# A memset after every row gather in both attention loops of a four-layer graph network, and constant waits in the counted layer

## The chip, the core and the metric

The kernel runs on one core of a Trainium2 chip. The metric is the device time of one execution in microseconds. The engines are TensorE (PE in the profile, PEld for its weight loads), VectorE (DVE), ScalarE (ACT), GpSimd (POOL) and SyncE (SP), each with an instruction stream of its own, in order, synchronised by semaphores.

## The reference, cut to what matters

Four graph layers, each on a layer-normed copy of x and added back to it. There are 3125 nodes with 128 features, and 103125 edges (50000 in both directions and a loop at each node), sorted by destination. Layer 0 is a two-step graph convolution, layer 3 filters 64 edge attributes and multiplies them with gathered rows. The change touches the loops of layers 1 and 2, and one place in layer 0.

```python
def reference(x, src, dst, edge_attr_64, ...):
    edge_index = jnp.stack([src, dst])
    h = jnp.maximum(_layernorm(x, axis=-1), 0.0)
    x = x + _L0_gnn_ref(h, edge_index, ...)
    ...
    x = x + _L1_gnn_ref(h, edge_index, ...)
    ...
    x = x + _L2_gnn_ref(h, edge_index, ...)
    ...
    x = x + _L3_gnn_ref(h, edge_attr_64, src, dst, ...)
    return x

def _L1_gnn_ref(x, edge_index, W, att):
    ...
    projected = (x @ W).reshape(N, HEADS, OUT_CH)
    src = projected[row]
    dst = projected[col]
    scores = jnp.tanh(src + dst)
    scores = jnp.einsum('ehc,hc->eh', scores, att)
    scores = jnp.exp(scores - jnp.max(scores, axis=0, keepdims=True))
    out = jax.ops.segment_sum(src * scores[:, :, None], col, num_segments=N)
    normalizer = jax.ops.segment_sum(scores, col, num_segments=N)
    out = out / jnp.maximum(normalizer, 1e-12)[:, :, None]
    ...

def _L2_gnn_ref(x, edge_index, gamma, beta, Wl, bl, Wr, br, att, res_W, bias):
    ...
    xl = (h @ Wl + bl).reshape(n, H, D)
    xr = (h @ Wr + br).reshape(n, H, D)
    src, dst = (edge_index[0], edge_index[1])
    e = jax.nn.leaky_relu(xl[src] + xr[dst], NEG_SLOPE)
    alpha = jnp.einsum('ehd,hd->eh', e, att)
    alpha = _segment_softmax(alpha, dst, n)
    msg = xl[src] * alpha[..., None]
    out = jax.ops.segment_sum(msg, dst, num_segments=n)
    ...
```

## The kernel before

The edges are cut into 202 tiles of 512 (`k.tiles`), each of four sub-tiles of 128 (`SUB`), one edge to a partition. The stages follow each other: the count matrices of layer 0 are built, layer 0 is computed from them (`sum_counted`), then come the additive attention of layer 1 and the GAT attention of layer 2 (both by `attend`), and the filtered scatter of layer 3 (`scatter_filtered`) with its dense layers.

**`attend`.** The projected node features lie in a table in HBM. GpSimd's block is unrolled (L2069 to L2073): for each tile it waits until a slot of the ring is free (`sums_ready`, `n + 1 - ring`) and then runs `gather` (L892), which issues four indirect DMAs, one per sub-tile, each of 128 rows by the source indices (L897). Each counts up its own semaphore `rows_loaded[slot][j]`. The ring has 12 slots in layer 1 (rows of 128 features) and 8 in layer 2 (rows of 256 features: two heads). The slots are tiles whose names differ, so the profile calls the target of a gather `gathered`, `wide` or `h_nm`. TensorE turns the gathered rows (L2088), adds the destination's features from a window of the table by a one-hot matrix (L2092), and ScalarE applies tanh (L2172) or a copy (L2170), in layer 2 followed by VectorE's leaky relu (L2221). TensorE forms the scores (L2109 in layer 1, L2106 in layer 2) and, beforehand, the cells' mask (L2101); VectorE takes the maximum of each row (L2228, L2230, in layer 2 also L2235), ScalarE the exponential (L2178), TensorE turns the weights back (L2119), VectorE copies them (L2246), and TensorE multiplies them with the gathered rows into the sums of each node in the tile's window (L2144 in layer 1, L2140 in layer 2), which counts up `sums_ready`. The sums are copied by ScalarE (L2190, or L2184 in layer 2, where TensorE turns them with L2152). VectorE makes the one-hot matrices (L1477); SyncE loads the destinations (L1457) and the windows (L1462). Each engine's order is written out, and its loop runs ahead of the others only as far as the semaphores let it.

**`sum_counted`.** The count matrices lie in HBM (`k.all_counts`), built in an earlier stage. One tile of them is built again here before the sums begin; the number of such rounds is `k.rebuild`, here 1. SyncE loads the first group of 24 matrices in three thirds, then stores the rebuilt tile (L1378), and then loads the next groups (L1390). TensorE multiplies each group with the features (L1195), 25 blocks of nodes; for the first group it waits for the thirds one by one.

**`scatter_filtered`** has for each sub-tile one indirect DMA that adds rows (L1709), 606 in all, each with a `sem_inc` and a wait of GpSimd ahead of it.

## Time and profile before

| | us |
|---|---|
| timed runs | 4901.65, 4906.43, 4910.76 |
| median | 4906.43 |
| span of the profiled execution | 4898.1 |
| busy in it: TensorE, VectorE, GpSimd, ScalarE | 3999.0, 2847.4, 2828.1, 1737.4 |
| from the first gather of layer 1 (668.90) to the end of its last | 1222.6 |
| from the first gather of layer 2 (2023.53) to the end of its last | 1305.4 |

The spans and busy times are of one profiled execution, the timed runs are others; the profiled span lies 8.3 us under their median. A row of the timeline gives start, duration, engine, line, operation, output and input, and in brackets how long the engine was idle before it and what ended that (`<-`); "issue" is the engine's own work between instructions, "remote" a semaphore event whose sender the profile could not name, and a release can also be put down to a DMA that happened to end then. Granted clock is TensorE's, as a share of its full 2.4 GHz.

### The profile page before, as it was taken

The page shows a single profiled execution, that of the slowest core. Times are in us where ns is not written, and L with a number is a line of the kernel's source. Part 1 is how long each engine was busy: PE and PEld are TensorE (multiplying, and loading weights), DVE is VectorE, ACT ScalarE, POOL GpSimd, SP SyncE. Part 2 cuts the span into 40 slices and gives each one's busy share as a digit, 9 for nine tenths or more (in the row PEclk, how much of TensorE's full clock was granted, in tenths as well). Part 3 has the DMA queues.
Part 4 walks back from the last instruction along what each step waited for, and adds up shares of the span by engine and source line. Part 5 has one row for each costly group of instructions (what it writes and reads, how often), then busy time and mean ns, then how long its engine had stood idle before and what let it go on. Part 6 is the DMA issues. An engine that isn't in the chain of part 4 may idle for free. (4 is left out here: it accounts for less than half of the span.)

```text
span 4898.1 us, 89702 instructions
## 1 busy us (share of the span) xinstructions
PE 3999.0 (82%) x22566; PEld 2260.3 (46%) x22566; DVE 2847.4 (58%) x8457; ACT 1737.4 (35%) x4474; POOL 2828.1 (58%) x3060
## 2 busy tenths in 40 slices
PE   3997927788887877488888888885399999999987
PEld 1344414445544544344444444442256655556652
DVE  7994032333333334555555555556678888888868
ACT  3773023344344334333333333331322222222227
POOL 0122356666666663555555555554368888888862
PEclk8998957776777777688988888886699999999999
DMA  2333422222222221333333333330056666666650
GB/s 80 91 87 103 147 71 57 57 56 57 57 56 57 56 57 27 113 98 96 97 97 96 96 97 96 97 96 18 21 97 104 105 105 104 104 105 104 104 110 13
DMA packets 377425, 402.41 MB, mean 82 GB/s; under 512 B 86457, under 2 KB 322502, under 8 KB 377030
## 3 DMA queue, kind: packets, MB, share of 16 engines
q0 software_dynamic: 151904, 198.72, 21.0%
q1 hardware_dynamic: 225382, 202.21, 14.4%
q8 instruction: 43, 0.70, 0.1%
q14 instruction: 96, 0.79, 0.1%
HBM read 312.91 MB, written 87.78 MB: 82 GB/s over the span
## 5 line engine op out<-in xcount | busy, mean ns | idle before, releaser
L897 POOL DMA_INDIRECT gathered<-table,sources x952 | 903.6, 949 | 600.6 <-issue 259.9
L1709 POOL DMA_INDIRECT sums<-gathered,idx x606 | 988.7, 1632 | 217.8 <-issue 166.4
L1571 PE MATMUL bank<-wide 128*128 128x512 bf16 x3636 | 851.5, 379 | 0.0
L2228 DVE TENSOR_REDUCE neg_raw<-bank 80x1 f32<-80x512 f32 (+1 forms) x404 | 276.6, 685 | 725.9 <-remote 252.1
L897 POOL DMA_INDIRECT wide<-table,sources x464 | 438.7, 946 | 275.1 <-issue 125.7
L1571 PEld LDWEIGHTS bank<-wide 128*128 128x128 bf16 x3636 | 347.7, 98 | 364.1 <-issue 1.7
L2178 ACT ACTIVATE msg<-bank,neg_top 80x512 f32<-80x512 f32 (+1 forms) x404 | 275.7, 682 | 643.1 <-DVE neg_top L2230 353.6
L1222 POOL TENSOR_TENSOR acc<-acc,msg 128x20 f32 x404 | 108.3, 268 | 411.2 <-issue 244.6
L2221 DVE TENSOR_TENSOR zact<-zact,bank 128x512 f32<-128x512 f32 x404 | 259.5, 683 | 123.1 <-ACT zact L2170 72.9
L2106 PE MATMUL bank<-zact,att_cells 128*32 128x512 f32 x808 | 289.4, 732 | 37.9 <-issue 36.2
L2088 PEld LDWEIGHTS bank<-ident,gathered 128*128 128x128 f32 x1360 | 191.8, 165 | 258.0 <-issue 232.2
L2109 PE MATMUL bank<-zact,att_cells 128*80 128x512 f32 x404 | 301.6, 838 | 6.6 <-issue 6.6
L2246 DVE COPY edge_rows<-bank 128x320 f32<-128x320 f32 (+1 forms) x404 | 183.2, 453 | 203.5 <-remote 132.7
L2144 PE MATMUL bank<-edge_rows,gathered 128*128 128x80 f32 x1088 | 193.9, 337 | 92.5 <-DVE edge_rows L2246 81.9
L2088 PE MATMUL bank<-ident,gathered 128*128 128x128 f32 x1360 | 237.4, 317 | 35.4 <-issue 26.4
L2119 PE MATMUL bank<-ident,msg 80*128 80x80 f32 (+1 forms) x1616 | 215.5, 262 | 61.5 <-issue 33.9
L897 POOL DMA_INDIRECT h_nm<-table,sources x200 | 189.4, 947 | 130.5 <-DMA wide<-table,sources 69.3
L2190 ACT COPY partial<-bank 32x20 f32 (+1 forms) x808 | 132.6, 164 | 357.5 <-remote 239.5
L1169 DVE TENSOR_SCALAR gathered<-iota_c,partial 128x500 f16<-128x500 f16 x808 | 257.6, 339 | 1.7 <-issue 1.3
L2170 ACT ACTIVATE zact<-bank 128x512 f32<-128x512 f32 x404 | 216.8, 588 | 98.1 <-DMA window<-parts 81.2
L1178 PE MATMUL bank<-gathered,zact 128*128 128x500 f16 x812 | 209.3, 381 | 49.4 <-ACT zact L1285 28.1
L1622 ACT COPY gathered<-bank 128x437 f32<-128x437 f32 x202 | 106.1, 525 | 337.0 <-PE bank L1597 249.7
(406 smaller groups left out, 7603.9 us busy)
## 6 DMA issues: line engine op xcount, KB each, us to landing
zact<-in_src_flat SPq DMA_DIRECT2D x202, 192.0 KB
edge_rows<-in_attr_rows SPq DMA_DIRECT2D x202, 128.0 KB
dst_pair<-local_rows SPq DMA_DIRECT2D x177, 128.0 KB
gathered<-table,sources POOLq DMA_INDIRECT x952
dst_pair<-local_rows SPq DMA_DIRECT2D x202, 64.0 KB
counts<-wide SPq DMA_DIRECT2D x4, 3000.0 KB
counts<-fm_ab SPq DMA_DIRECT2D x4, 3000.0 KB
fm_ab<-counts SPq DMA_DIRECT2D x4, 3000.0 KB, 11.0
```

Of the source, the lines that this page charges most:

```text
L897: pool.indirect_dma_start(out=g[:, j, :], out_offset=None, in_=table, in_offset=bass.IndirectOffsetOnAxis(ap=mine, axis=0)).then_inc(rows_ ...
L1169: hot = dve.tensor_scalar(k.cell_hot[slot][:, j, :], k.iota_c[:, :], own, None, ALU.is_equal)
L1571: pe.matmul(k.bank[b][:, :], k.split[t.two][:, c, :], k.source_hot[t.two][:, b * CHUNK:(b + 1) * CHUNK], start=first, stop=c == PARTS - 1, ...
L1709: pool.indirect_dma_start(out=k.sums[j], out_offset=bass.IndirectOffsetOnAxis(ap=k.idx[t.slot][:, j:j + 1], axis=0), in_=out_rows(t)[:, j, ...
L2088: pe.matmul(z_bank(t, h)[:, j * P:(j + 1) * P], g[:, j, h * F:(h + 1) * F], k.ident[:, :], is_transpose=True, start=(j == 0), stop=False, ...
L2106: mm = pe.matmul(score_bank(t)[own_cells(h), :], a.att[h][:, own_cells(h)], k.zact[t.two][:, h, :], start=False, stop=True, skip_group_che ...
L2109: mm = pe.matmul(score_bank(t), a.att[0][:, :], k.zact[t.two][:, 0, :], start=False, stop=True)
L2119: mm = pe.transpose(weight_bank(t)[:, j * cells:(j + 1) * cells], raised(t)[:, j * P:(j + 1) * P], k.ident[lanes(t), lanes(t)])
L2170: act.mul(k.zact[t.two][:, h, :], z_bank(t, h)[:, :], 0.2).then_inc(slope_ready, 1)
L2178: act.activation(raised(t), score_bank(t), ACT.Exp, bias=k.neg_top[lanes(t), bass.ds(t.t, 1)], accum_out=k.weight_sum[lanes(t), bass.ds(t. ...
L2221: m = dve.tensor_tensor(za, za, z_bank(t, h)[:, :], ALU.max)
L2228: dve.tensor_reduce(raw, score_bank(t), AX.X, ALU.max, negate=True).then_inc(top_found, 1)
```

## The change

First, both attention loops hand `gather` a new semaphore `paused`. After each of the four indirect DMAs of a tile GpSimd now sets one of eight columns of a new tile `pause` (128x8, fp16), which nothing reads, to zero, and counts `paused` up; from the third tile on, `gather` first waits for the memsets of the tile two before, which wrote the same columns. It adds 4 memsets a tile, 808 to each loop. `gather` has no other callers.

Second, in `sum_counted` SyncE loads only the first two thirds inside the loop of rebuilt tiles, waits at the loop's end for the second of them, and loads the third after the loop. TensorE waits inside its loop for the first third, then for a new semaphore `second_there` and for a count of 16, where it waited against `k.rebuild * 16 + 16`, a register's value.

```diff
@@ gather
-def gather(k, pool, table, g, gathers_begun, rows_loaded, t):
+def gather(k, pool, table, g, gathers_begun, rows_loaded, t, paused=None):
 
     pool.sem_inc(gathers_begun, 1)
+    if paused and t.t > 1:
+        pool.wait_ge(paused, (t.t - 1) * SUB)
     for j in range(SUB):
         mine = k.sources[:, t.t * SUB + j:t.t * SUB + j + 1]
         pool.indirect_dma_start(out=g[:, j, :], out_offset=None, in_=table,
                                 in_offset=bass.IndirectOffsetOnAxis(ap=mine, axis=0)
                                 ).then_inc(rows_loaded[t.slot][j], 16)
+        if paused:
+            at = t.t % 2 * SUB + j
+            pool.memset(k.pause[:, at:at + 1], 0.0).then_inc(paused, 1)
@@ sum_counted, SyncE
-                    for landed in begun:
+                    for landed in begun[0:2]:
                         sp.sem_inc(landed, 16)
+
+                    def load_third(i):
+                        lo, hi = thirds[i]
+                        sp.dma_start(k.counts[0][:, lo:hi, :], k.all_counts[lo:hi, :, :].rearrange(
+                            "t p c -> p t c")).then_inc(begun[i], 16)
                     with sp.Fori(0, k.rebuild) as n:
-                        for (lo, hi), landed in zip(thirds, begun):
-                            sp.wait_ge(landed, n * 16 + 16)
-                            sp.dma_start(k.counts[0][:, lo:hi, :], k.all_counts[lo:hi, :, :].rearrange(
-                                "t p c -> p t c")).then_inc(landed, 16)
+                        for i in range(2):
+                            sp.wait_ge(begun[i], n * 16 + 16)
+                            load_third(i)
                         sp.wait_ge(evicted, n + 1)
...
                         sp.wait_ge(stored, n * 16 + 16)
                         sp.sem_inc(free, 1)
+                        sp.wait_ge(begun[1], n * 16 + 32)
+                        sp.sem_inc(rounds_done, 1)
+                    sp.sem_inc(second_there, 1)
+                    load_third(2)
@@ sum_counted, TensorE
                         cell_counts(k, pe, 0, k.bank[0]).then_inc(counted, 1)
+                        pe.wait_ge(begun[0], n * 16 + 32)
...
                         for i, (lo, hi) in enumerate(thirds if first(now) else [(0, now.size)]):
-                            if first(now):
-                                pe.wait_ge(begun[i], k.rebuild * 16 + 16)
+                            if first(now) and i == 1:
+                                pe.wait_ge(second_there, 1)
+                            if first(now) and i == 2:
+                                pe.wait_ge(begun[2], 16)
@@ attend
+        paused = st.sem("paused")
...
-                    gather(k, pool, table, rows(t), gathers_begun, rows_loaded, t)
+                    gather(k, pool, table, rows(t), gathers_begun, rows_loaded, t, paused)
```

GpSimd's instructions in the additive loop before, where the ring goes from one set of slots to the next. The name in brackets is that of an earlier holder of the same semaphore: `parts0_rounded2` is `sums_ready` here.

```order
716 L897 DMA gathered<-table,sources 128x128 [waits parts0_rounded2]
717 L897 DMA gathered<-table,sources 128x128 x3
718 L897 DMA wide<-table,sources 128x128 [waits parts0_rounded2]
719 L897 DMA wide<-table,sources 128x128 x3
720 L897 DMA wide<-table,sources 128x128 [waits parts0_rounded2]
721 L897 DMA wide<-table,sources 128x128 x3
```

The same loop after the change; `parts0_rounded0` is `sums_ready`, `build_low_ready` is `paused`.

```order
820 L900 DMA gathered<-table,sources 128x128 [waits parts0_rounded0,build_low_ready]
821 L905 MEMSET pause 128x1
822 L900 DMA gathered<-table,sources 128x128
823 L905 MEMSET pause 128x1
824 L900 DMA gathered<-table,sources 128x128
825 L905 MEMSET pause 128x1
826 L900 DMA gathered<-table,sources 128x128
827 L905 MEMSET pause 128x1
828 L900 DMA gathered<-table,sources 128x128 [waits parts0_rounded0,build_low_ready]
```

Each gather, the last of a tile too, is followed by one memset, and the two waits stand together before a tile's first gather.

SyncE's instructions at the rebuild loop of `sum_counted` before (L1375 the thirds, L1378 the store, L1390 the next group).

```order
48 L1375 DMA wide<-counts 128x8x500 [waits counted_begun0]
49 L1375 DMA wide<-counts 128x8x500 [waits counted_begun1]
50 L1375 DMA wide<-counts 128x8x500 [waits counted_begun2]
51 L1377 REGISTER_ALU
52 L1378 ISA [waits counted_evicted]
53 L1378 DMA counts<-fm_ab 128x500
54 L1372 REGISTER_ALU [waits counted_stored]
55 L1372 COMPARE_AND_BRANCH
56 L1390 DMA fm_ab<-counts 128x24x500
```

And after it (L1382 the thirds, L1389 the store, L1405 the next group):

```order
48 L1382 DMA wide<-counts 128x8x500 [waits counted_begun0]
49 L1382 DMA wide<-counts 128x8x500 [waits counted_begun1]
50 L1388 REGISTER_ALU
51 L1389 ISA [waits counted_evicted]
52 L1389 DMA counts<-fm_ab 128x500
53 L1393 REGISTER_ALU [waits counted_stored]
54 L1384 REGISTER_ALU [waits counted_begun1]
55 L1384 COMPARE_AND_BRANCH
56 L1382 DMA wide<-counts 128x8x500
57 L1405 DMA fm_ab<-counts 128x24x500
```

The third load has moved from before the store to behind the loop, directly ahead of the next group's load.

## Rows read from the trace of the kernel before

**Rows 1.** The page, its first line.
```profile
span 4898.1 us, 89702 instructions
```

**Rows 2.** Windows: length, busy us (instructions) of PE, PEld, DVE, ACT, POOL, granted clock, DMA share, GB/s.
```profile
668.90:1891.53 1222.63, 965.56 (x4112) 582.91 (x4113) 392.16 (x1255) 472.89 (x1465) 766.40 (x808) 0.72 0.22 57
2020.00:3330.00 1310.00, 1081.83 (x7479) 567.60 (x7480) 722.54 (x1977) 406.80 (x994) 765.76 (x809) 0.86 0.33 96
3700.00:4600.00 900.00, 900.00 (x5429) 540.30 (x5428) 738.27 (x1861) 264.57 (x621) 758.26 (x466) 1.00 0.65 104
```

**Rows 3.** The timeline of GpSimd, first and last gather of the GAT loop.
```profile
2023.53 1.54 POOL L897 DMA_INDIRECT gathered<-table,sources  x1 [3.10 <-POOLq L539]
...
3328.03 0.94 POOL L897 DMA_INDIRECT gathered<-table,sources  x1 [0.30 <-issue]
```

**Rows 4.** The page, groups: count | busy us, mean ns | idle us before, releaser.
```profile
L897 POOL DMA_INDIRECT gathered<-table,sources x952 | 903.6, 949 | 600.6 <-issue 259.9
...
L897 POOL DMA_INDIRECT wide<-table,sources x464 | 438.7, 946 | 275.1 <-issue 125.7
...
L897 POOL DMA_INDIRECT h_nm<-table,sources x200 | 189.4, 947 | 130.5 <-DMA wide<-table,sources 69.3
```

**Rows 5.** The timeline at the opening of the additive loop.
```profile
708.58 0.77 PE L2119 MATMUL bank<-ident,msg 80*128 80x80 f32 x4 [5.49 <-issue]
...
732.82 0.49 DVE L2246 COPY edge_rows<-bank 128x320 f32<-128x320 f32 x1 [25.19 <-remote]
```

**Rows 6.** The timeline of a burst in the additive loop.
```profile
1320.67 1.09 PE L2109 MATMUL bank<-zact,att_cells 128*80 128x512 f32 x2
...
1327.61 0.94 POOL L897 DMA_INDIRECT gathered<-table,sources  x1 [0.30 <-issue]
1328.73 0.69 DVE L2228 TENSOR_REDUCE neg_raw<-bank 80x1 f32<-80x512 f32 x1 [8.48 <-remote]
...
1331.79 0.94 POOL L897 DMA_INDIRECT gathered<-table,sources  x1 [3.23 <-remote]
```

**Rows 7.** The timeline of a burst in the GAT loop.
```profile
2146.62 1.07 PE L2140 MATMUL bank<-gathered,edge_rows 128*32 128x128 f32 x16
...
2149.75 0.95 POOL L897 DMA_INDIRECT gathered<-table,sources  x1 [0.30 <-issue]
...
2151.81 0.26 ACT L2184 COPY tile_rows<-bank 64x128 f32<-64x128 f32 x1 [3.39 <-DMA wide<-table,sources]
```

**Rows 8.** The timeline in the scatter stage of the last layer.
```profile
3998.25 0.91 PE L1597 MATMUL bank<-msg,gathered 128*128 128x128 f32 x6
...
3999.20 0.53 ACT L1622 COPY gathered<-bank 128x437 f32<-128x437 f32 x1 [1.54 <-PE bank L1597]
```

**Rows 9.** The timeline of GpSimd in the prologue.
```profile
0.35 0.10 POOL L3154 MEMSET const-float32-0.0<- 128x1 f32 x1
0.38 0.10 POOL L3154 MEMSET const-float32-1.0<- 128x1 f32 x1
```

**Rows 10.** A window of 7 us in the additive loop, columns as in rows 2.
```profile
1204.00:1211.00 7.00, 7.00 (x23) 3.98 (x23) 0.02 (x1) 2.52 (x6) 5.48 (x6) 0.50 0.21 56
```

**Rows 11.** The timeline of TensorE in that window.
```profile
1204.59 1.99 PE L2109 MATMUL bank<-zact,att_cells 128*80 128x512 f32 x2
...
1210.91 2.00 PE L2109 MATMUL bank<-zact,att_cells 128*80 128x512 f32 x2
```

**Rows 12.** The timeline at the start of the counted sums.
```profile
465.09 0.37 SPq L1390 DMA_DIRECT2D fm_ab<-counts  x1
465.17 0.45 PE L1195 MATMUL bank<-wide,h_nm 128*128 128x160 f16 x2 [6.74 <-SPq L1387]
...
482.82 0.56 ACT L1210 COPY msg<-bank 128x480 f32<-128x480 f32 x1 [23.78 <-PE bank L1195]
```

**Rows 13.** DMA issues of that stage: count, KB each, median us to landing.
```profile
wide<-counts SPq DMA_DIRECT2D x3, 1000.0 KB, 7.7
```

**Rows 14.** The one-hots of the GAT loop: duration min/median/max in ns, first and last start.
```profile
L1477 DVE TENSOR_SCALAR onehot_t<-dst_pair,iota_w,always x97: 398/413/620, 2204.3 to 3191.3; 128x512 bf16<-128x512 bf16 x97
```

More of the change, by code:

```diff
@@ L309, in load_everything @@
     k.att1 = k.sb("att1", [F, HEADS1])
+    k.pause = k.sb("pause", [P, 2 * SUB], FP16)
     one, two = k.soft1, k.soft2
@@ L1356, in one_pass @@
             loaded, begun = [st.sem(f"loaded{i}") for i in range(2)], [st.sem(f"begun{i}") for i in range(3)]
+            second_there, rounds_done = st.sem("second_there"), st.sem("rounds_done")
             summed, kept, adds_begun, added = st.sem("summed"), st.sem("kept"), st.sem("adds_begun"), st.sem("added")
```

## Prediction, made before the changed kernel ran

> **What bounds the kernel now.** The page gives the span, 4898.1 us [rows 1]; the median of the three timed runs is 4906.43, so 8.3 us lie outside the profiled span, and I add them at the end. The stretches come next [rows 2]. The additive loop takes 1222.6 us and the GAT loop 1305.4 us (2023.53 to the end of its last gather at 3328.97 [rows 3]), together 52% of the span. In neither is an engine full: TensorE is busy 965.56 of 1222.63 and 1081.83 of 1310.00 us, GpSimd 766.40 and 765.76. In the last layer's edge stage it is 900.00 of 900.00. So the two loops wait on something, and only they are touched by the memset.
>
> The groups of the page show what GpSimd could do [rows 4]. The 1616 gathers of both loops take 949, 946 and 947 ns each. Before one that follows another without a wait there are 0.30 us of issue [rows 3]. So a gather costs 1.25 us, a tile of four 5.0 us, and 808 gathers 1010 us. The idle time before them is 600.6 + 275.1 + 130.5 = 1006.2 us; less 1616 x 0.30 = 485 it leaves 521 us of waiting. By loop: 1222.6 - 1010 = 212 and 1305.4 - 1010 = 295, 507 in all; the rest lies before the first gather of each loop and in rounding.
>
> What GpSimd waits for is `sums_ready`, the signal that TensorE has finished with a slot of gathered rows. TensorE is not late with its work; its signals are late. At the opening of the additive loop 12 tiles, 48 gathers, run without a wait from 668.9 to 668.9 + 48 x 1.25 = 729. TensorE ends the four turns of the first weights (L2119) at 708.58 + 0.77 = 709.35; the copy that needs just these (DVE L2246) starts at 732.82, 23.5 us later, 3.8 us after the burst's end [rows 5]. In the steady loop the score matmul L2109 ends at 1321.76, the maximum that reads it (DVE L2228) starts at 1328.73, again just after the last gather of a burst (1328.55), and GpSimd itself waits 3.23 us more [rows 6]. In the GAT loop L2140 ends at 2147.69, its copy on ScalarE starts at 2151.81, 1.1 us after the burst of gathers ended at 2150.70 [rows 7]. In the scatter stage it is not so: L1597 ends at 3999.16 and ScalarE's copy of it starts at 3999.20 [rows 8], while scatters go out all the time. There a `sem_inc` and a wait stand before each scatter, and 466 of them in 900 us are 1.93 us apart [rows 2]. My reading: a run of gathers without a break holds TensorE's signals up, the consumers idle, and their lateness stops GpSimd in turn. That this is the run of gathers and not the gathers as such is inferred from these four places.
>
> **The memset, part by part.** It adds 808 memsets of 128x1 to each loop, 1616 in all, and before each tile from the third on a wait for memsets of the tile two before; those are older on the same in-order engine, so that wait is met when it is reached, and the queue behind it (the gathers, for which TensorE's feature transposes wait) is not held by it. The nearest rows for a memset are those of the prologue: 0.10 us long, the next one starting 0.03 later [rows 9]. I bound the added GpSimd time by these: 1616 x 0.03 = 48 us, 1616 x 0.10 = 162 us. I take 0.10, since a memset between two gathers has no second memset to overlap; a gather then costs 1.35, a tile 5.4 us, a loop 1091 us. The Trainium skill (Perfetto Trace Analysis, Per-instruction lifecycle) says that a GpSimd instruction's span in a profile is unreliable and that it is to be timed by the start-to-start spacing; by that, the price is the 0.03, and the added time 48 us. No row here has a memset between gathers, so the sum keeps both ends. Neither end is below nothing by itself; the gain can only come through the signals.
>
> If the signals become prompt, GpSimd is the bound: additive 1222.6 - 1091 = 132 us, GAT 1305.4 - 1091 = 214 us, 346 us together. Two things take from that. First TensorE's clock in the additive loop: granted 0.72 on average [rows 2], and where it is at its low level, 1.2 GHz, granted 0.50, a tile of TensorE takes 6.32 us, 1204.59 to 1210.91 [rows 10, 11], more than the 5.4 of GpSimd; the loop goes between the levels. The full clock would carry it, the low one not, and I see no row that says that the share of either changes. I take half of the 132, about 70 us. Second the GAT loop: TensorE is busy 1081.83 us of it at 0.86, just under 1091, so small stalls on either engine no longer hide behind the other. I take 175 of the 214. Sum: 70 + 175 = 245 us.
>
> **The mend in the counted layer** is run once here (`k.rebuild` is 1). Before, SyncE issues all three thirds of the first counts, then stores the rebuilt tile. After it, the third one goes out after the store has landed, just before the next group's load at 465.09, and TensorE's start at 465.17 stands behind one more issue and one semaphore step, some 0.4 us by the 0.37 of such an issue [rows 12]. A third is 1000 KB and lands in 7.7 us [rows 13]: at 465.2 + 7.7 = 473. TensorE works the first group from 465.17 to about 482.8, where ScalarE's copy starts after its wait [rows 12], 17.6 us, so it wants the last third after two thirds of that, 11.7 us, at 477. Four us of cover; were it gone, the loss is what lands late, and twice the landing time would still cost under 4 us. The new waits of TensorE for loads that landed long before cost nothing. I take 1 us. So 245 - 1 = 244: span 4654, time 4654 + 8.3 = 4662.
>
> **Rivals.**
> A. *No relief, longer bursts.* The memset is again GpSimd work, and if the signals come only when GpSimd's queue stops, each burst just grows. The cycle is then burst plus gap, as in rows 5 to 7, where signals came 1 to 4 us after the burst's end, and each gather's memset stands in it: 1616 x 0.03 = +48 (4954), 1616 x 0.10 = +162 (5068). This is the side that loses; it decides if the held signals come out of order with the gathers only in GpSimd's waits. For it: the 0.30 us of issue between two gathers are a gap already three times as long as the memset, and they don't let the signals out. Against it: that gap is the same instruction stream preparing the next gather, whereas a memset is work of another kind; the scatters at 1.93 us with their own step before each hold nothing up [rows 8].
> B. *Relief paid back in full.* A memset must be started and finished between gathers; if that costs 0.3 us, as an issue does, a tile is 4 x 1.55 = 6.2 us, a loop 1252: additive +30, GAT -53, together -23 with prompt signals, nothing to speak of; at 0.35 exactly zero. Within 0.2%: 4897 to 4916.
> C. *Partial relief.* The signals come out at some memsets, the bursts of the opening break up, and a third to a half of the waits go: 4760 to 4890.
> D. *Vector shuts GpSimd out.* The memset wants to write SBUF while DVE runs its one-hot in bf16, 0.41 us each [rows 14], 404 of them; if each held up GpSimd fully, +166 beyond A, 5234. Against: the same DVE instructions already run beside the gathers, whose means are 949, 946 and 947 ns with nothing added. The Trainium skill (SBUF, Who interferes with whom) says that DVE in a 2-port mode and GpSimd lock each other out, and that a GpSimd DMA's descriptor writes are held too; the trace shows no such stretch in the gathers.
>
> **How the numbers follow.** Prompt signals with GpSimd near its bound: .45, at 4662, with a range of its own from 4550 (346 us and a memset of 0.10) to 4760. C .12; B, with the case that the memset does nothing at all, .10; A .30; D or something dearer .03. Below 4550 the memset would have to be 0.03 with nothing lost to the clock. The likeliest is 4662. The range must leave out no more than 2 in 10, and A has .30 in it, so it goes to A's end: 4550 to 5070. A measurement of this kernel tells about 0.2% from no change, 10 us. Faster .57, same .10, slower .33.
>
> **What would show it.** In the trace after: the start-to-start of two gathers with a memset between them (1.35 by me; 1.28, 1.55 or more by the others) and the waiting before gathers (521 us to nearly nothing; unchanged in A). DVE L2246 in the opening of the additive loop no longer 23 us behind L2119; L2228 and ScalarE's L2184 within some tenths of TensorE's end. The loops' lengths, 1150 and 1130 us by me. The granted clock of the additive loop: if it falls below 0.72 while GpSimd waits for real, my half was too much. Rows in which the signals are prompt and GpSimd still waits would put the bound elsewhere. The counted layer's first matmul within 1 us of 465.2. My number is wrong above all if a memset is no break for the signals.

## The result, and the profile after

The changed kernel took 4912.69 us (median of 18 runs) against 4904.99 us of the kernel before (18 runs): a ratio of 1.0016, 95% interval [1.001, 1.0022]. It is 0.16% slower, which is no change by the 0.2% of the prediction. The forecast of 4662 us was wrong; the direction it gave .57 to did not come.

The windows of the changed kernel over its two loops (columns as in rows 2, each from about the first gather to the last memset):

```profile
span 4902.5 us, 91319 instructions
```
```profile
668.00:1889.00 1221.00, 921.39 (x4092) 553.97 (x4093) 391.44 (x1249) 470.81 (x1460) 863.60 (x1616) 0.76 0.22 57
2024.00:3336.00 1312.00, 1079.26 (x7484) 568.57 (x7485) 721.31 (x1974) 406.87 (x994) 865.73 (x1616) 0.86 0.33 96
```

All 1616 memsets ran, 808 in each loop, and the loops took 1221 and 1312 us where they had taken 1222.6 and 1305.4 [rows 2, 3]. The groups of GpSimd's gathers (page), which answer rows 4:

```profile
L900 POOL DMA_INDIRECT gathered<-table,sources x952 | 903.8, 949 | 478.0 <-issue 151.5
...
L900 POOL DMA_INDIRECT wide<-table,sources x464 | 438.9, 946 | 224.0 <-issue 75.2
...
L900 POOL DMA_INDIRECT h_nm<-table,sources x200 | 189.2, 946 | 108.8 <-DMA wide<-table,sources 71.3
```

The idle time before the gathers is 478.0 + 224.0 + 108.8 = 811 us instead of 1006. The 195 us between them are the memsets, not less waiting. GpSimd's timeline in a stretch without waits shows it:

```profile
673.80 0.94 POOL L900 DMA_INDIRECT gathered<-table,sources  x1 [0.19 <-issue]
674.74 0.13 POOL L905 MEMSET pause<- 128x1 f16 x1
675.05 0.94 POOL L900 DMA_INDIRECT gathered<-table,sources  x1 [0.19 <-issue]
```

Two gathers start 1.25 us apart, as before. The memset takes 0.12 us of the 0.30 us that lay between two gathers anyway, and 0.18 stay. Here it is neither a cost nor a pause. That holds for nearly all gathers, not for every one: within a tile the gathers of this trace start 1.265 us (additive loop) and 1.268 us (GAT loop) apart on average, against 1.261 and 1.262 before. Some of the stretched ones lie in the opening burst, where each of the five gathers from 701.3 on has the next one only 1.4 to 2.1 us later, though no wait for `sums_ready` stands there yet:

```profile
703.29 0.94 POOL L900 DMA_INDIRECT gathered<-table,sources  x1 [0.81 <-issue]
...
705.39 0.94 POOL L900 DMA_INDIRECT gathered<-table,sources  x1 [0.81 <-POOL pause L905]
```

The second one is put down to the memset, that is to `paused`. At the opening of the additive loop TensorE's signals are still late:

```profile
690.79 0.69 PE L2138 MATMUL bank<-ident,msg 80*128 80x80 f32 x4
...
707.72 0.77 PE L2138 MATMUL bank<-ident,msg 80*128 80x80 f32 x4 [5.49 <-issue]
...
716.65 0.49 DVE L2265 COPY edge_rows<-bank 128x320 f32<-128x320 f32 x1 [9.89 <-remote]
```

The copy at 716.65 is the first of the loop, and it waits for the first turns alone. Those are the turns at 690.79, which end at 691.48; the ones at 707.72 are the second tile's, which TensorE may do ahead. So the first signal comes 716.65 - 691.48 = 25.2 us late. In the kernel before the first turns are these:

```profile
691.75 0.79 PE L2119 MATMUL bank<-ident,msg 80*128 80x80 f32 x4
```

They end at 692.54, and the first copy starts at 732.82 [rows 5]: 40.3 us late. The prediction took the second tile's turns (708.58) for the first ones and so read 23.5. Something moved at that place, then, in the one trace of each, and the loop's length did not. In the steady loops, worked out from all semaphore events in the trace that can be matched to a TensorE instruction, about two thirds of TensorE's signals of the additive loop and half of those of the GAT loop come over 0.3 us after the instruction's end, before and after alike. On average over all they are 1.6 to 2.7 us late; this is a floor, since an update is counted from the last instruction of its semaphore that had ended.

In the counted layer the first sums start earlier than in rows 12, not later (463.09 against 465.17):

```profile
463.09 0.45 PE L1201 MATMUL bank<-wide,h_nm 128*128 128x160 f16 x2 [4.42 <-SPq L1402]
...
481.86 0.56 ACT L1216 COPY msg<-bank 128x480 f32<-128x480 f32 x1 [22.58 <-PE bank L1201]
```

The store of the rebuilt tile was over sooner. From its issue to the next load there are 2.6 to 3.4 us in the traces of all kernels with the mend (here 459.55 to 462.62), and 5.8 us in that of the kernel before (459.32 to 465.09), where the third load had gone out ahead of the store. That the two shared the transfers there is the likely reason and was not tried. The group takes 481.86 - 463.09 = 18.8 us instead of 17.6, so it ends 1 us earlier where the prediction had 1 us later.

### The profile page after: what moved, and what is told of

Its sections match the earlier page's. It is cut to its first block and busy times, and to the rows that moved or that the text cites. A ratio compares the mean times of both kernels' runs of the same rounds, so it can differ in the third digit from the quotient of the medians.

```text
span 4902.5 us, 91319 instructions
## 1 busy us (share of the span) xinstructions
PE 3956.5 (81%) x22566; PEld 2234.6 (46%) x22566; DVE 2849.0 (58%) x8457; ACT 1736.7 (35%) x4474; POOL 3026.9 (62%) x4676
## 5 line engine op out<-in xcount | busy, mean ns | idle before, releaser
L900 POOL DMA_INDIRECT gathered<-table,sources x952 | 903.8, 949 | 478.0 <-issue 151.5
L900 POOL DMA_INDIRECT wide<-table,sources x464 | 438.9, 946 | 224.0 <-issue 75.2
L2125 PE MATMUL bank<-zact,att_cells 128*32 128x512 f32 x808 | 276.8, 752 | 24.7 <-issue 24.2
L2128 PE MATMUL bank<-zact,att_cells 128*80 128x512 f32 x404 | 291.1, 811 | 6.9 <-issue 6.8
L2163 PE MATMUL bank<-edge_rows,gathered 128*128 128x80 f32 x1088 | 182.9, 323 | 115.3 <-DVE edge_rows L2265 82.3
L900 POOL DMA_INDIRECT h_nm<-table,sources x200 | 189.2, 946 | 108.8 <-DMA wide<-table,sources 71.3
L2203 ACT COPY tile_rows<-bank 64x128 f32<-64x128 f32 x202 | 52.0, 258 | 541.6 <-DMA wide<-table,sources 524.5
```

Source lines behind the costliest of these rows:

```text
L900: pool.indirect_dma_start(out=g[:, j, :], out_offset=None, in_=table, in_offset=bass.IndirectOffsetOnAxis(ap=mine, axis=0)).then_inc(rows_ ...
L2125: mm = pe.matmul(score_bank(t)[own_cells(h), :], a.att[h][:, own_cells(h)], k.zact[t.two][:, h, :], start=False, stop=True, skip_group_che ...
L2128: mm = pe.matmul(score_bank(t), a.att[0][:, :], k.zact[t.two][:, 0, :], start=False, stop=True)
```

## The experiments

The kernels were run in five sessions, each with its own runs of the kernel before. In three sessions that took 4906.2, 4907.1 and 4939.6 us, in two others 4382.8 and 4383.2 us. This is the main finding, and so every experiment is told with the kernel before of its own session. I call a session late when the kernel before took over 4900 us and prompt when it took 4383; a signal is called late when the semaphore update comes over 0.3 us after the end of the instruction that sends it. The record gives sessions 1 and 2 the same chip number, so the chip alone does not seem to decide it.

| session | kernel before, us | experiment: ratio to it, 95% interval |
|---|---|---|
| 1, late | 4906.2 | mend_only 0.9993 [0.9983, 1.0002]; wait_each 1.0035 [1.0021, 1.0049]; long_tile 0.9933 [0.9917, 0.9948] |
| 2, prompt | 4382.8 | long_each 1.2377 [1.2352, 1.2402]; window_two 1.0959 [1.0941, 1.0977]; half_tile 1.0306 [1.0289, 1.0323]; double_tile 1.1356 [1.1337, 1.1375] |
| 3, prompt | 4383.2 | after_again 0.9989 [0.9979, 0.9999]; mend_again 0.9997 [0.9987, 1.0006]; half_again 1.0298 [1.0281, 1.0315]; window_again 1.0979 [1.0960, 1.0997] |
| 4, late | 4907.1 | window_third 0.9891 [0.9875, 0.9908]; long_each_again 1.1052 [1.1029, 1.1074]; quarter_each 0.9874 [0.9858, 0.9891] |
| 5, late | 4939.6 | half_third 0.9976 [0.9966, 0.9987]; each_500 1.0168 [1.0140, 1.0195]; three_of_four 0.8902 [0.8877, 0.8928] |

All kernels but three_of_four compute the whole, and all have the mend of the counted layer. For the memsets without the mend (memset_only) there is no result. The diffs are against the changed kernel, cut at the dots.

### The mend alone: mend_only, mend_again

```diff
-                    gather(k, pool, table, rows(t), gathers_begun, rows_loaded, t, paused)
+                    gather(k, pool, table, rows(t), gathers_begun, rows_loaded, t)
```

> Only the counted layer's mend of the change, no memset. If the measured 0.16% (7.7 us) of the change comes from the mend, this is 4 to 8 us slower than the kernel before. If it comes from the memsets, this is within 2 us of it; the trace of the changed kernel has the first counted sums starting earlier, not later, than before, so I expect 0 to 1 us faster.

> The mend of the counted layer alone, here as a stand-in for the kernel before with a trace from the same chip and session as the others: within 0.1% of the kernel before in either case. With prompt signals its loops are 808 x 1.25 = 1010 us each and no gather but the first ones waits; with late signals 1220 and 1306 us.

Measured 4901.47 us against 4906.2, and 4380.88 against 4383.2. The mend costs nothing in either. That leaves the changed kernel's 0.16% to the memsets, which is inferred and not measured, since they were not run alone; by one trace of each, 6 us of it are in the GAT loop (1312 against 1306 us).

These two runs are the same program in a late and a prompt session, so they show what the two conditions are. First the late one (windows over the loops, then groups of the page and the issues' row, whose last number, if there is one, is the time to the landing):

```profile
667.00:1886.00 1219.00, 939.92 (x4094) 565.23 (x4094) 389.39 (x1243) 471.09 (x1453) 766.46 (x808) 0.74 0.22 57
2025.00:3333.00 1308.00, 1083.03 (x7485) 567.83 (x7485) 721.34 (x1973) 405.54 (x994) 765.19 (x808) 0.87 0.33 96
```
```profile
L900 POOL DMA_INDIRECT gathered<-table,sources x952 | 903.5, 949 | 603.4 <-issue 264.1
...
L2264 DVE COPY edge_rows<-bank 128x320 f32<-128x320 f32 (+1 forms) x404 | 183.3, 454 | 252.7 <-remote 184.6
...
gathered<-table,sources POOLq DMA_INDIRECT x952
```

And the same of mend_again, in the prompt session:

```profile
667.00:1682.00 1015.00, 904.06 (x4202) 518.37 (x4203) 413.89 (x1295) 498.03 (x1496) 767.28 (x808) 0.84 0.27 69
1798.00:2815.00 1017.00, 947.91 (x7557) 509.94 (x7557) 733.17 (x1998) 424.45 (x1005) 768.12 (x808) 0.98 0.44 124
```
```profile
L900 POOL DMA_INDIRECT gathered<-table,sources x952 | 903.9, 949 | 299.3 <-issue 293.8
...
L2264 DVE COPY edge_rows<-bank 128x320 f32<-128x320 f32 (+1 forms) x404 | 183.3, 454 | 152.2 <-PE bank L2137 143.9
...
gathered<-table,sources POOLq DMA_INDIRECT x952, 2.6
```

The loops are 1015 and 1017 us, which is little more than 808 x 1.25 = 1010: GpSimd alone. Of the 521 us between the two traces' spans, 495 lie in these windows and 23 between the two loops (1886 to 2025 against 1682 to 1798); what stands before the first loop and after the second differs by 3 us. Nothing waits for `sums_ready` (299.3 us idle are the 0.30 us of issue, 952 times). VectorE's copy is released by TensorE's turns themselves and no longer by "remote". At the opening the first copy follows the first turns within 0.04 us:

```profile
691.11 0.78 PE L2137 MATMUL bank<-ident,msg 80*128 80x80 f32 x4
691.92 0.49 DVE L2264 COPY edge_rows<-bank 128x320 f32<-128x320 f32 x1 [2.95 <-PE bank L2137]
```

In the late trace of the same program it starts 39.3 us after them. A gather itself is the same 949 ns. The late trace has no landing time for the gathers, the prompt one 2.6 us: in the late trace many semaphore events are missing, of all engines and of the transfers, 24415 DMA landing events in the whole trace against 58702. Missing events are a mark of a late session, not of late signals: of the last layer, which takes the same time in both, some 14400 landing events are recorded against 22400, and the signals of its scatter stage are prompt. The record has a traced span for every execution, late and prompt, so whether the recording of events has a part in the lateness is a rival that no run here tests. What makes a session late is not known; the program is the same, and the executions of one session agree within 0.5%.

### A wait between the gathers: wait_each

```diff
-    if paused and t.t > 1:
-        pool.wait_ge(paused, (t.t - 1) * SUB)
...
+        if t.t > 0:
+            n, ring = t.t - 1, len(rows_loaded)
+            pool.wait_ge(rows_loaded[n % ring][j], (n // ring + 1) * 16)
+        pool.sem_inc(paused, 1)
         pool.indirect_dma_start(out=g[:, j, :], out_offset=None, in_=table,
...
-        if paused:
-            at = t.t % 2 * SUB + j
-            pool.memset(k.pause[:, at:at + 1], 0.0).then_inc(paused, 1)
```

> No memset; ahead of each gather a semaphore increment by GpSimd and a wait for the gather of the same sub-tile one tile before to have landed, in form what the scatter stage has. Landings come 1.5 to 1.8 us after a gather's end, the wait is for one four gathers (5 us) back, so it is met. If a wait or an increment between two gathers is what lets TensorE's signals out (as in the scatter stage), the loops shorten by up to 400 us together. If it is the density of gathers that holds them, nothing changes but 0.05 to 0.1 us a gather of GpSimd's issue: 0 to 100 us slower, or hidden.

Measured 0.35% slower, late session; 0.69 of TensorE's signals are late in the additive loop and 0.55 in the GAT loop, as without the waits (0.69 and 0.54 in mend_only). A semaphore increment and a wait that is met do not let the signals out. So they are not what keeps the scatter stage free of late signals.

### One pause per tile: long_tile, half_tile, half_again, half_third, double_tile

```diff
-    k.pause = k.sb("pause", [P, 2 * SUB], FP16)
+    k.pause = k.sb("pause", [P, 800], mybir.dt.uint8)
...
-    if paused and t.t > 1:
-        pool.wait_ge(paused, (t.t - 1) * SUB)
...
-        if paused:
-            at = t.t % 2 * SUB + j
-            pool.memset(k.pause[:, at:at + 1], 0.0).then_inc(paused, 1)
+        if paused and j in (3,):
+            done = t.t * 1 + (3,).index(j)
+            if done:
+                pool.wait_ge(paused, done)
+            pool.memset(k.pause[:, :], 0.0).then_inc(paused, 1)
```

(That is long_tile. 400 columns in half_tile and its repeats half_again and half_third; two memsets of 800 in double_tile. The wait is for the memset before, on the same engine.)

> One memset of 128x800 bytes after the last gather of each tile instead of a small one after each gather, so some 0.7 us (by the 0.86 ns a column of the 2x3200 memset: 2.75 us) in which no gather is issued. GpSimd then needs about 5.0 + 0.7 = 5.7 us a tile against 6.05 and 6.46 us now. If a stop of that length lets the signals out, the loops fall to 5.7 us a tile: 70 + 150 = 220 us faster. If the signals only come when GpSimd has been still for over 1 us after a gather, or at the landing, nothing is let out and the pauses add to the bursts: 2 x 202 x 0.7 = up to 280 us slower, less where they fall into GpSimd's own waits.

> One memset of 128x400 bytes (about 0.4 us) after the last gather of a tile; the 128x800 of 0.78 us gave 35.7 us. If the gain goes by whether a pause is longer than the 0.30 us between two gathers at all, this gives the same 36 us or more, since it costs GpSimd less. If it goes by the length of the pause, half or less: 0 to 18 us faster.

> Two memsets of 128x800 bytes after the last gather of a tile, 1.6 us of pause; a tile costs GpSimd 5.0 + 1.6 = 6.6 us, above the 6.0 and 6.4 us of now. In long_tile most late signals came out either within 0.75 us or from 1.0 us after the last gather's end. If a pause of 1.6 us lets all out, no other waits of GpSimd remain and the loops are 202 x 6.6 = 1333 us each: 115 + 30 = 145 us slower than before, with VectorE's remote waits gone. If the signals are let out by something else, they are still late and it is slower still, 200 us or more.

> The 0.4 us pause per tile again. With prompt signals it cost 134 us, 2 x 202 x 0.34, as GpSimd's bound says. With late signals: by the theory that the length of the pause counts, 0 to 18 us faster; by the theory that any pause over 0.30 us helps, 36 us or more faster.

> A 0.4 us pause per tile. With late signals in the session and a limit of one gather in 1.50 us: the additive loop takes 1210 us, the GAT loop 1285 as with the longer pause, 20 to 40 us faster than the kernel before. With prompt signals 134 us slower, as twice before.

GpSimd's timeline of long_tile gives the price of a pause:

```profile
1200.59 0.94 POOL L898 DMA_INDIRECT gathered<-table,sources  x1 [0.30 <-issue]
1201.53 0.78 POOL L905 MEMSET pause<- 128x800 uint8 x1
1202.48 0.95 POOL L898 DMA_INDIRECT gathered<-table,sources  x1 [0.17 <-issue]
```

The two gathers are 1.89 us apart: 0.94 + 0.78 + 0.17. That is 0.64 over 1.25, so a memset costs GpSimd its length less about 0.14 us. The pause of 0.78 us gained 36 us in a late session, against 220 expected; the additive loop took 1210 us and the GAT loop 1285. half_third gained 0.24%, 11 us. The longer pause gained more, but neither lets the signals out: 0.72 and 0.61 of them are late in long_tile (additive and GAT loop), 0.71 and 0.52 in half_third. In the prompt sessions every pause is paid in full: half_tile and half_again cost 134 and 127 us. For double_tile the expectation was written against a late session; in the prompt one its 596 us are the 2 x 202 x (2 x 0.78 - 0.12) = 582 us that GpSimd's bound gives.

### At most two gathers under way: window_two, window_again, window_third

```diff
-    if paused and t.t > 1:
-        pool.wait_ge(paused, (t.t - 1) * SUB)
...
+        n, ring = t.t * SUB + j - 2, len(rows_loaded)
+        if n >= 0:
+            pool.wait_ge(rows_loaded[n // SUB % ring][n % SUB], (n // SUB // ring + 1) * 16)
         pool.indirect_dma_start(out=g[:, j, :], out_offset=None, in_=table,
...
-        if paused:
-            at = t.t % 2 * SUB + j
-            pool.memset(k.pause[:, at:at + 1], 0.0).then_inc(paused, 1)
```

> No memset; each gather waits until the gather two before it has landed, so never more than two are under way. A landing comes 1.5 to 1.8 us after a gather's end and two gathers take 2.5 us, so the pitch becomes about 1.3 us in the additive loop and 1.4 in GAT, a tile 5.2 and 5.6 us. If it is the backlog of transfers under way that holds the signals up, they come prompt: the loops fall to some 1070 and 1130 us, 300 us faster. If it is GpSimd's own work of issuing, whatever is in flight, the signals stay late and this is 20 us faster to 80 us slower, since the gathers after a burst's pause are at most moved.

> At most two gathers under way, again. With prompt signals it cost 419 us (loops of 1188 and 1251 us). With late signals: if the backlog of transfers holds the signals, they come prompt here and the time is the same some 4800 us, 100 us faster than the kernel before; if issuing holds them, they are late and it is 100 us slower or more.

> At most two gathers under way. If the session has late signals (the kernel before at some 4906 us): were it the backlog of transfers that holds them, they come prompt and this takes the 4800 us that it takes with prompt signals, 100 us under the kernel before; were it the issuing, they stay late, and this is 100 us or more over it. If the session has prompt signals it repeats the 1.097.

In the prompt sessions the waits cost 419 and 432 us: the landing takes longer than my 1.3 and 1.4 us of pitch assumed, and the loops of window_two are 1188 and 1251 us long. In the late session it is 1.1% faster than the kernel before, 4852 us; the loops are 1214 and 1265 us, near those of the prompt sessions. TensorE's signals are still late there, about as often in the additive loop (two thirds), less in the GAT loop (some 0.4, and by 0.5 us on average instead of 1.8). The waits also move the gathers apart, to 1.43 and 1.56 us at the median, so this does not tell fewer transfers under way from a lower density; neither frees the signals here.

### A pause after every gather: long_each, long_each_again, quarter_each, each_500

As long_tile, but after every gather, with 800, 300 and 500 columns.

> A memset of 128x800 bytes (0.78 us as measured) after every gather, so gathers start some 2.0 us apart, like the scatters of the last layer (1.93). Theory of the density: at that pitch TensorE's signals are prompt throughout, VectorE's and ScalarE's remote waits are gone, and the loops are bound by GpSimd alone: 808 x 2.0 = 1620 us each, so 400 + 310 = 710 us slower in all. Theory of the kind of instruction (gathers hold the signals, scatters do not): signals late still, and GpSimd waits besides, over 900 us slower.

> 0.78 us of memset after every gather, gathers 1.9 us apart as the scatters of the last layer are. With late signals in the session: were it the density of gathers, all signals are prompt and the time is the 5425 us of the prompt session, since GpSimd is the bound in both; were it gathers as such, the loops are longer than 808 x 1.90 = 1535 us each.

> A memset of 128x300 bytes after every gather, some 0.30 us long. Two gathers are 0.30 us apart of which the 0.12 us memset took its time without moving the next start, so by the theory that a memset is hidden in the issue time of the next gather the pitch rises only by what it goes over some 0.3 us less the 0.19 left of issue: to 1.35 to 1.45 us a gather. With prompt signals 1616 x 0.10 to 0.20 = 160 to 320 us slower. With late signals, if it is the pitch that lets them out, it gains: GpSimd's 5.6 us a tile against 6.05 and 6.46, up to 200 us faster; if not, 0 to 320 us slower.

> A memset of 128x500 bytes, about 0.53 us, after every gather, so that gathers are 1.65 us apart. If there is a limit of one gather in 1.50 us, all signals are prompt here in a session with late signals, GpSimd waits for nothing and each loop takes 808 x 1.65 = 1333 us, so 111 + 28 = 140 us slower than the kernel before. If gathers at any pitch below 1.9 us hold signals up, the loops are longer than that. With prompt signals: the same loops, and 646 us slower than a kernel before of 4383.

The gathers were 1.89, 1.48 and 1.64 us apart at the median. For the last two, from quarter_each and each_500:

```profile
1199.23 0.95 POOL L898 DMA_INDIRECT gathered<-table,sources  x1 [0.17 <-issue]
1200.18 0.36 POOL L905 MEMSET pause<- 128x300 uint8 x1
1200.71 0.95 POOL L898 DMA_INDIRECT gathered<-table,sources  x1 [0.17 <-issue]
```
```profile
1199.27 0.95 POOL L898 DMA_INDIRECT gathered<-table,sources  x1 [0.17 <-issue]
1200.20 0.54 POOL L905 MEMSET pause<- 128x500 uint8 x1
1200.91 0.95 POOL L898 DMA_INDIRECT gathered<-table,sources  x1 [0.17 <-issue]
```

long_each took 5424.55 us in the prompt session and 5423.09 in the late one, the same time, where the kernels before of the two sessions are 524 us apart. At that pitch the two conditions do not differ in time, the signals of TensorE that are recorded come within 0.03 us in both, and GpSimd is the bound (808 x 1.89 = 1527). The loops of long_each_again, late session:

```profile
674.00:2208.00 1534.00, 1265.88 (x4210) 705.24 (x4210) 522.04 (x1296) 510.35 (x1505) 1400.21 (x1615) 0.58 0.18 46
2327.00:3860.00 1533.00, 1222.96 (x7553) 594.23 (x7553) 889.98 (x1994) 424.04 (x1005) 1399.61 (x1616) 0.80 0.29 82
```

Its trace still lacks events of a late session (40634 landing events against 59153 of long_each). each_500, late session, windows over its loops and two groups:

```profile
674.00:2011.00 1337.00, 1150.28 (x4209) 647.30 (x4210) 433.63 (x1293) 502.38 (x1503) 1204.16 (x1616) 0.67 0.20 52
2134.00:3467.00 1333.00, 1092.75 (x7557) 552.96 (x7557) 757.07 (x1997) 424.63 (x1007) 1199.49 (x1616) 0.88 0.33 94
```
```profile
L898 POOL DMA_INDIRECT gathered<-table,sources x952 | 908.7, 955 | 165.8 <-issue 160.7
...
gathered<-table,sources POOLq DMA_INDIRECT x952, 2.5
```

The expectation was 1333 us for each loop, with all signals prompt. Nothing but issue is idle before the gathers, and of TensorE's recorded signals under 3% are late in the GAT loop and none in the additive one. The whole came 85 us slower, where 140 were expected: the kernel before took 33 us longer in session 5 than in the other late ones, for no reason that is known. Of 1.64 us there is no run in a prompt session. quarter_each is between:

```profile
666.00:1881.00 1215.00, 1004.93 (x4114) 587.03 (x4115) 420.04 (x1252) 483.18 (x1461) 1067.98 (x1616) 0.73 0.22 58
2014.00:3283.00 1269.00, 1062.62 (x7496) 568.88 (x7498) 767.41 (x1980) 414.58 (x999) 1067.46 (x1616) 0.86 0.35 99
```

At a pitch of 1.48 us the opening of the additive loop has prompt signals throughout (at 1.25 the first signal was 40.3 us late), but from some 200 us into the loop two thirds are late again. Still it is the fastest of the whole kernels in a late session: 4847 us, 1.3% under the kernel before. So in a late session the border lies between 1.48 and 1.64 us a gather, where the loops of the kernel before average 1222.6 / 808 = 1.51 and 1305.4 / 808 = 1.62.

### One gather in four left out: three_of_four

```diff
-    for j in range(SUB):
+    for j in range(SUB - 1):
         mine = k.sources[:, t.t * SUB + j:t.t * SUB + j + 1]
...
-                        pe.wait_ge(rows_loaded[t.slot][j], (t.rounds + 1) * 16)
+                        if j < SUB - 1:
+                            pe.wait_ge(rows_loaded[t.slot][j], (t.rounds + 1) * 16)
```

(TensorE reads `g[:, min(j, 2)]` in the features and the sums.)

> No memset, and the fourth gather of every tile left out (its edges use the third one's rows, so the output is another one); all other work is done. GpSimd needs 3.75 us a tile. With late signals: if the limit is one gather in 1.50 us, it no longer binds at 4.5 us a tile, TensorE is the bound, and the loops fall to 4.7 to 5.2 us a tile, 950 to 1050 us, 450 us faster. If the limit is one on a tile's other signals and loads, the additive loop stays at 1210 us. With prompt signals: TensorE's own bound shows, by the same measure 0 to 60 us under the kernel before.

Late session, windows over its loops:

```profile
674.00:1659.00 985.00, 850.62 (x4101) 519.63 (x4101) 393.01 (x1251) 471.54 (x1461) 576.65 (x606) 0.82 0.22 57
1791.00:2841.00 1050.00, 945.78 (x7486) 518.39 (x7487) 723.08 (x1975) 408.74 (x994) 573.25 (x606) 0.97 0.33 94
```

538 us faster with a quarter of the gathers gone, more than the 450 expected: 985 and 1050 us, 4.88 and 5.20 us a tile. The late loops' length hangs on the number of gathers; a limit by a tile's other signals and loads, which would have left the additive loop at 1210 us, is excluded. But 0.56 and 0.38 of TensorE's signals are still late here, by 1.4 and 0.9 us on average over all, though only one gather in 1.63 and 1.73 us goes out on average. So a mean rate below the border does not suffice; the gathers still go in bursts at 1.25 us.

### after_again

> The changed kernel once more, since the kernel before has shown two times, 4906 us with the signals of TensorE late and 4383 us with all of them prompt. With the signals late: 0.1 to 0.2% above the kernel before, as measured. With them prompt GpSimd is the bound, a gather costs 1.25 us with or without the memset (the memset fills the issue time between two gathers), so 0 to 0.2% slower than a kernel before of 4383 us; a memset that cost 0.1 us would show as 160 us here.

Measured 4378.22 us against 4383.2, a ratio of 0.9989 [0.9979, 0.9999]. The memset is free here, where GpSimd is the bound through both loops and every 0.01 us of it would show: 1616 x 0.10 us would have been 3.7%. Within a tile its gathers start 1.251 and 1.254 us apart on average, those of mend_again 1.253 and 1.257.

## Why the prediction was wrong, step by step

**Right:** the reading of the bound. TensorE's signals, not TensorE, hold the two loops; 507 us of waiting were worked out from rows 2 to 4, and the prompt sessions show the kernel without them: 4383 us, 523 us less, with loops of 1015 and 1017 us. Two of its four places were read one tile off, and both were later than it says: the first signal at the opening by 40.3 us and not 23.5, and in rows 6 the maximum at 1328.73 reads the scores that ended at 1318.33, not those of 1321.76, so it is 10.4 us behind them and not 7.0. The mend at nothing was right (mend_only, mend_again), the direction of its 1 us not.

**Wrong, the step that failed: that a memset between two gathers breaks the run that holds the signals.** The prediction inferred from four places that "a run of gathers without a break holds TensorE's signals up" and gave .45 to a memset being such a break; the 245 us of its sum rest on it, and they came to nothing. The runs show two conditions instead, both needed. One is the session: in a prompt one the same unbroken run at 1.25 us a gather holds nothing up (mend_again). The other, in a late session, is density: the signals are prompt at 1.89 and 1.64 us a gather, late at 1.48 and 1.25; a wait between gathers frees nothing (17 us slower), a pause of 0.4 or 0.78 us a tile gains 11 or 36 us. All three larger distances were made with memsets of different length; the waits of window_third, which part the gathers by other means, fit them, and no run separates distance from the length of the memset further. In rows 8 it was not the `sem_inc` and wait that kept the signals prompt: wait_each has both and is late. The 1.93 us between scatters fit the density; that they are why was not tried in that stage.

**Wrong, a size: the memset's price.** I took 0.10 us, 162 us in all, between 0.03 and 0.10. It was 0 where GpSimd is the bound (after_again): a memset takes its place in the 0.30 us of issue between two gathers, and of the longer ones only what goes beyond 0.12 to 0.15 us costs. The argument "a memset between two gathers has no second memset to overlap" looked at the wrong partner; it overlaps the issue of the next gather. The 0.30 us stood in rows 3 as idle time, and I used it as a gap only in rival A. The rule of the Trainium skill (Perfetto Trace Analysis, Per-instruction lifecycle), by which a GpSimd span is not to be trusted and start-to-start spacing is, named the right measure; the spacing to look at was that of the gathers, 1.25 us with and without. It also follows that such a memset can't be a pause to anything that goes by the distance of two gathers, since it does not lengthen it.

**The rivals.** What came is the tail of rival B, "the case that the memset does nothing at all", .10 together. That the time stayed inside the stated range is therefore owed to the range reaching to A's end, not to the mechanism of the forecast. A (longer bursts, +48 to +162 us) was right that there is no relief and failed on the price. B's sum has a slip: with 1.60 us a gather (0.35 for the memset) its two loops come to 2 x 1293 us, 58 more than before; the zero is at 0.31. C was seen at the opening alone, where the first lateness is 25.2 us against 40.3 and nothing came of it; that the memsets did it is not shown, since the same place varies between late traces that have none (39.3 us in mend_only, 29.5 in three_of_four). D showed nothing: the gathers take 949, 946 and 946 ns. The half of the additive loop that I took off for the clock was needless in the prompt sessions: there the granted clock is 0.84 instead of 0.74, and the loop runs at GpSimd's pace. With memsets at no cost, the signals prompt and neither deduction, the sum would have been the whole 507 us. The 4550 of the prediction is 4560 by its own terms, 4906 - 346.

**The remaining 7.7 us.** In the late sessions the changed kernel is 0.16% above the kernel before, with 6 us in the GAT loop; in the prompt session it is 0.11% below. By the starts of all gathers in one trace of each, 4 of the 6 us are gathers of one tile that start later than 1.25 us after the one before (10.7 us of it against 7.1 before); why they do is open. Open as well is what makes a session late, whether the recording of events has a part in it, and what in a gather does it: its sixteen landing signals, its descriptors or its reads. three_of_four and the pitches show that it goes by gathers and their distance; no run took these apart.

## What to carry to other kernels

Before inserting work as a pause, look at the start-to-start distance of the instructions around it: what fits into the issue time costs nothing and separates nothing. When a signal comes late and the instruction that sends it does not, vary the rate of what seems to disturb it before its form. A gain or loss of a pause that was measured under such a disturbance can turn round without it: quarter_each is 1.3% faster than its kernel before in a late session, and by its 1.48 us a gather against 1.25 it would be some 2 x 808 x 0.23 = 370 us slower in a prompt one, an estimate; the pause of half_tile, measured in both, goes from -0.2% (half_third) to +3%. Neither is a version to keep.

## What the runs showed of the hardware

The same program has two times, 4906 and 4383 us, by session and not by execution, and 495 of the 521 us between two traces of it lie in two loops of dense indirect gathers. In the slower condition TensorE's semaphore updates come late in these loops, the first one 39 to 41 us (kernel before, mend_only, wait_each), while the recorded ones of VectorE, ScalarE and GpSimd come within 0.02 us (kernel before, mend_only). Its traces also lack many events (24415 against 58702 DMA landing events), in stages with prompt signals too. At 1.89 us a gather the two conditions take the same time; at 1.64, measured in the slower one alone, the signals are prompt. A GpSimd memset of 0.12 us between two indirect DMAs costs nothing, and longer ones cost their length less 0.12 to 0.15 us: 1.25, 1.48, 1.64 and 1.89 us from gather to gather for memsets of 0.12, 0.36, 0.54 and 0.78 us.
